# Transformer layer with routed experts: the first expert layer moves from expert order to token order

## The reference

```python
xn = layernorm(x)
# attention, linear, 16 heads of 16
q, k = elu(xn @ Wq + bq) + 1, elu(xn @ Wk + bk) + 1
v = xn @ Wv + bv
kv = einsum('bkhd,bkhm->bhdm', k, v)
att = (einsum('bqhd,bhdm->bqhm', q, kv) / max(sum_k(q . k), 1e-6)) @ Wo + bo
# feed-forward: a shared part for every token ...
swiglu = lambda x: silu(x[..., :512]) * x[..., 512:]
shared = swiglu(xn @ w_in.T) @ w_out.T
# ... and a routed part: one first layer for all experts, two of 8 second layers for each token
h = swiglu(xn @ w1.T)                      # 8192 x 512
w_se = top2(softmax(masked expert logits) * group probability)
routed = sum_e (h * w_se[:, e]) @ w2[e].T  # 8192 x 256
out = x + att + shared + routed
```

## Time and profile before

| | us |
|---|---|
| median of 3 runs | 1070.78 |
| lowest and highest run | 1067.65, 1071.2 |
| the profiled execution, its own time | 1058.75 |
| its span, first to last instruction | 1056.8 |
| stage one ends on PE (last matmul of `y`) | about 609.8 |
| first expert matmul of stage two | 612.65 |

### The profile page before, as it was taken

The page is one execution under the profiler, slowest core; times in us unless marked ns, Lnnn a source line. Parts: engine busy times, 40 slices in busy tenths (PEclk is TensorE's granted clock), DMA queues, the critical chain, the costliest instruction groups (busy, mean ns, idle before and its releaser), DMA issues.

```text
span 1056.8 us, 21589 instructions
## 1 busy us (share of the span) xinstructions
PE 1012.4 (96%) x6662; PEld 910.4 (86%) x6663; DVE 672.9 (64%) x1681; ACT 398.8 (38%) x676; POOL 491.5 (47%) x489
## 2 busy tenths in 40 slices
PE   5999999999999999999999889999999999999996
PEld 5889879888888888898888779999999999999996
DVE  7887797788779778877977634444443444444343
ACT  3454354345445444544444322222222222222221
POOL 5343343534343443334344445555555555555534
PEclk9999999999999999999999899999999999999999
DMA  8012111201211120211111032222222122222321
GB/s 269 24 53 73 52 40 52 72 20 57 68 52 40 52 72 26 64 54 52 40 52 53 12 82 71 64 72 61 69 69 71 63 69 69 63 68 69 65 45 21
DMA packets 55585, 64.55 MB, mean 61 GB/s; under 512 B 18829, under 2 KB 45581, under 8 KB 55568
## 3 DMA queue, kind: packets, MB, share of 16 engines
q1 hardware_dynamic: 42624, 35.86, 11.3%
q0 software_dynamic: 12944, 28.47, 9.9%
HBM read 37.16 MB, written 28.58 MB: 62 GB/s over the span
## 4 chain that ended last, share of the span: by engine, by line
PE 60%; DVE 22%; issue 12%; ACT 3%; DMA 1%; POOL 1%; SPq 0%; DVEq 0%; ACTq 0%; POOLq 0%
PE bank L309 19%; PE bank L310 19%; PE bank L311 18%; DVE xn L715 4%; PE bank L381 3%; DVE stats L701 2%; DVE gated L795 1%; DVE lmax L726 1%; DVE phiq L825 1%; DVE phik L808 1%; PE bank L502 1%; ACT expt L617 1%; ACT expt L619 1%; ACT gated L598 1%; DVE rn L857 1%
## 5 line engine op out<-in xcount | busy, mean ns | idle before, releaser
L598 ACT ACTIVATE gated<-bank 128x512 f32<-128x512 f32 (+1 forms) x140 | 83.0, 593 | 264.2 <-PE bank L311 224.6
L309 PE MATMUL bank<-wexp_hi,h_hi 128*128 x600 | 170.2, 284 | 0.3 <-DVE h_lo L961 0.3
L310 PE MATMUL bank<-wexp_lo,h_hi 128*128 x600 | 168.5, 281 | 0.0
L311 PE MATMUL bank<-wexp_hi,h_lo 128*128 x600 | 168.5, 281 | 0.0
L997 POOL TENSOR_TENSOR h_lo<-gated,h_hi 128x512 fp32r<-128x512 f32 x64 | 83.8, 1309 | 170.5 <-ACT h_hi L602 169.0
L602 ACT CAST h_hi<-gated 128x512 fp32r<-128x512 f32 (+1 forms) x140 | 86.4, 617 | 159.1 <-DVE gated L795 158.4
L795 DVE TENSOR_TENSOR gated<-gated,bank 128x512 f32<-128x512 f32 (+1 forms) x140 | 95.2, 680 | 77.5 <-ACT gated L598 77.5
L971 DVE SCALAR_TENSOR_TENSOR res<-bank,cur,res 128x256 f32<-128x256 f32 x150 | 62.2, 477 | 123.1 <-PE bank L311 120.7
L1058 POOL DMA_INDIRECT out<-res,idx_cur x75 | 74.2, 989 | 102.9 <-DVE res L971 88.9
L309 PE MATMUL bank<-xnT_hi,wexp_hi 128*128 128x512 f32 (+1 forms) x304 | 117.7, 387 | 1.0 <-DVE xnT_lo L952 1.0
L310 PE MATMUL bank<-xnT_lo,wexp_hi 128*128 128x512 f32 (+1 forms) x304 | 117.7, 387 | 0.0
(11 more groups left out here) (171 smaller groups left out, 2506.6 us busy)
## 6 DMA issues: line engine op xcount, KB each, us to landing
xt<-x SPq DMA_DIRECT2D x16, 512.0 KB, 3.6
xn_d<-xn SPq DMA_DIRECT2D x16, 512.0 KB, 2.9
base_d<-res SPq DMA_DIRECT2D x16, 512.0 KB, 4.5
wstage<-w_exp SPq DMA_DIRECT2D x16, 320.0 KB, 4.2
tab_d<-wexp_hi SPq DMA_DIRECT2D x12, 128.0 KB, 5.5
phik<-tab_d SPq DMA_DIRECT2D x76, 2.0 KB
xn<-xn_d,idx_next POOLq DMA_INDIRECT x76, 2.8
res<-base_d,idx_cur POOLq DMA_INDIRECT x76
```

The lines of the kernel that those rows point to most:

```text
L309: e.matmul(to, w_hi, m_hi_, start=first_, stop=False, skip_group_check=free)
L310: e.matmul(to, w_hi, m_lo_, start=False, stop=False, skip_group_check=free)
L311: return e.matmul(to, w_lo, m_hi_, start=False, stop=last_, skip_group_check=free)
L598: act.activation(gated[:, j % 2, 0:cols], bank[gate_bank][:, 0:cols], ACT.Silu).then_inc(sil, 1)
```

## The change

The routed first layer is taken in stage one, in token order, from the transposed tokens that are there already (`routed`, four tiles of 12 matmuls with 512 columns for each sequence). Its gated result (128 x 512 fp32 for a tile) is scattered by POOL to `h_d` in HBM in expert-pair order, with the same positions as the table's rows. The residual + attention + shared part goes straight to the output, in token order. Stage two has only the second layer left: for each tile SP reads the tile's 128 rows of `h_d` in four DMAs, one for each band of 32 partitions, such that a block transpose on DVE (32 x 32 blocks) leaves the whole tile transposed; ACT rounds it, DVE makes the low part, PE takes 24 matmuls of 256 columns, DVE multiplies and adds the two results, and POOL scatters them to the output with an adding DMA. The groups have eight tiles, with one PSUM bank each; there are again 75 tiles. The normaliser of the attention is kept with heads on the partitions (32 rows for each tile), which does away with four transposes, one ACT copy and the shape of the last steps. `xn` shares its memory with `xt`; the residual is loaded a second time into `res`. `table_rows` and the layer norm's statistics come before the third gate on DVE. Tiles' padding rows are zeroed in `h_d` between the stages by 13 DMAs. Cut to its core:

```diff
+    h_d = nc.dram_tensor("h_d", (ROWS, H1), f32, kind="Internal").ap()
...
+        xn = xt
...
+        hs = [phik[:, 0:2, :].rearrange("p t d -> p (t d)"), phik[:, 2:4, :].rearrange("p t d -> p (t d)"),
+              expt[:, 0, :], expt[:, 1, :]]
...
+            def load(b, last):
...
+                    sp.wait_ge(t_done, DC * (b + 1))
+                    sp.dma_start(xt[:, :, :], x_rows(b + 1)).then_inc(x_ld, 16)
...
+                    wait_apart(sp, base_rdy, DC * b)
+                    sp.dma_start(out_rows(b - 1), res[:, :, :]).then_inc(base_st, 16)
+                    wait_apart(sp, base_st, 16 * b)
+                sp.dma_start(res[:, :, :], x_rows(b)).then_inc(r_ld, 16)
+                if first_row(b):
+                    sp.wait_ge(wexp_split, 1)
...
+            def tiles_in(q):
+
+                wait_apart(sp, tab_ld, 16 * TB * q)
+                at = [sp.value_load(info_i[0:1, 2, bass.ds(q * TB + t, 1)], min_val=0, max_val=SENT) for t in range(TB)]
...
+                    sp.dma_start(tab[:, bass.ds(q * TB + t, 1), :].rearrange("p t w -> p (t w)"),
...
+                    wait_apart(sp, tr_done, TB * q + t - 3)
+                    for i in range(4):
+                        sp.dma_start(hb[t][32 * i:32 * i + 32, :].rearrange("p (b f) -> p b f", b=TB),
+                                     h_d[bass.ds(at[t], P), i * P:(i + 1) * P].rearrange("(b p) f -> p b f", b=TB)).then_inc(h_ld[t], 16)
...
+            def routed(t, banks):
+
+                for half in range(2):
+                    for c in range(DC):
+                        mm = mm3(pe, bank[banks[half]][:, :], xnT_hi[:, c, t * P:(t + 1) * P], xnT_lo[:, c, t * P:(t + 1) * P],
+                                 w1_hi[:, c, half * H1:(half + 1) * H1], w1_lo[:, c, half * H1:(half + 1) * H1], c == 0, c == DC - 1)
+                mm.then_inc(rh_done, 1)
...
+
+                hidden(3, (3, 7))
+
+                pe.wait_ge(rsil_rdy, TB * b + 1)
+                pe.wait_ge(rg_rdy, TB * b + 1)
+                routed(1, (0, 1))
+
+                pe.wait_ge(rn_rdy, b + 1)
+                for c in range(DC):
+                    mm = pe.matmul(bank[(6, 2)[c]][:, :], spread[:, c, :], qn_hi[:, 1, :], start=True, stop=True)
+                    mm.then_inc(nb_done, 1)
+
+                pe.wait_ge(sil_rdy, HC * (b + 1))
+                pe.wait_ge(gate_rdy, HC * (b + 1))
...
+                routed(3, (0, 1))
+
+                pe.wait_ge(mlo_rdy, b + 1)
+                pe.wait_ge(qn_rdy, DC * (b + 1))
...
+                    transposes(b + 1)
...
+                tiles = LAST_TILES if last else GT
+                for t in range(tiles):
+                    at = [pe.value_load(info_i[0:1, n, bass.ds(g * GT + t, 1)], min_val=0, max_val=(E - 1) * HC * D)
+                          for n in range(2)]
+                    wait(pe, ysum, GT * g + t - 7)
+                    if first_row(g) and t in (5, 6):
+                        pe.wait_ge(base_rdy, DC * B - 6 + t)
+                    pe.wait_ge(tlo2, GT * g + t + 1)
...
+                        for j in range(HC):
+                            off = at[n] + (W1 + j * D)
...
+                high(b, 2)
+                act.wait_ge(acc_done, b + 1)
+                act.wait_ge(phiq_rdy, DC * (b + 1))
+                routed_silu(b, 0, 0)
+                act.wait_ge(m_done, b + 1)
+                act.copy(m_hi[:, :, :].rearrange("p c n -> p (c n)"), bank[4][:, :]).then_inc(mhi_rdy, 1)
+                silu(b, 3, 3)
+                high(b, 3)
+                routed_silu(b, 1, 0)
...
+                ranks_in(b)
...
+                table_rows(b)
                 if not last:
-                    gate(1, HC * b + 1, 1, sil_rdy, gate_rdy)
...
+                routed_gate(b, 0, 1)
...
+                if not last:
+                    normalise(b + 1)
+                gate(b, 3, 7)
+                if last:
+                    tile_list()
+                routed_gate(b, 1, 1)
...
+                routed_gate(b, 2, 7)
...
+                routed_gate(b, 3, 1)
...
+            def transposed(t, g):
+
+                dve.wait_ge(h_ld[t % TB], 64 * (2 * g + t // TB + 1))
+                wait(dve, tlo2, GT * g + t - 1)
+                dve.transpose(hT[t % 2].rearrange("p j (b k) -> p b j k", b=TB),
+                              hb[t % TB].rearrange("p (b j k) -> p b j k", b=TB, j=HC)).then_inc(tr_done, 1)
+
+            def low(t, g):
+
+                dve.wait_ge(thi2, GT * g + t + 1)
...
+                    wait(dve, out_st[t], 16 * g)
+                    dve.wait_ge(cur_rdy, 2 * g + t // TB + 1)
+                    dve.wait_ge(sw_done, GT * g + t + 1)
+                    add(t, g, 0)
+                    ahead(low, t + 3, g, last)
+                    dve.wait_ge(ystep, GT * g + t + 1)
+                    add(t, g, 1)
+                    ahead(transposed, t + 4, g, last)
...
+                def scatter(d, src, t, done):
+                    pool.indirect_dma_start(d, bass.IndirectOffsetOnAxis(ap=pos_i[:, t:t + 1], axis=0), src, None).then_inc(done, 16)
...
+                low(1, HC * b + 1, hhi_rdy, hlo_rdy)
                 if not last:
                     reciprocal_root(b + 1)
...
+                for t in range(TB):
+                    scatter(tab_d, rows[:, t, :], t, row_st)
                 low(2, HC * b + 2, hhi_rdy, hlo_rdy)
+                wait_apart(pool, rg_rdy, TB * b + 1)
+                scatter(h_d, hs[0], 0, hs_st)
                 low(3, HC * b + 3, hhi_rdy, hlo_rdy)
-                if not last:
-                    table_out()
+                for t in range(1, TB):
+                    wait_apart(pool, rg_rdy, TB * b + t + 1)
+                    scatter(h_d, hs[t], t, hs_st)
...
+            def scatter(g, half, tiles=TB):
+                wait_apart(pool, idxc_rdy, 2 * g + half + 1)
+                for t in range(TB * half, TB * half + tiles):
+                    wait_apart(pool, ysum, GT * g + t + 1)
+                    pool.indirect_dma_start(out, bass.IndirectOffsetOnAxis(ap=idx_cur[:, half, t % TB:t % TB + 1], axis=0), ring[t], None,
+                                            bounds_check=N - 1, oob_is_err=False, compute_op=ALU.add).then_inc(out_st[t], 16)
...
+            def group(g, last):
+                if last:
+                    scatter(g, 0, LAST_TILES)
+                else:
+                    entries(g, 1)
+                    scatter(g, 0)
+                    entries(g + 1, 0)
+                    scatter(g, 1)
```

More of the change, by code:

```diff
@@ new lines, in _ @@
+            rounds(sp, load, B)
+            sp.wait_ge(zero_set, 1)
+            sp.wait_ge(ends_rdy, 1)
+            for n in range(NCLS + 1):
+                if n < NCLS:
+                    g, k = divmod(n, NCLS // 2)
+                    j, i = PAIRS[k]
+                    end = sp.value_load(ends[0:1, 16 * g + 4 * j + i:16 * g + 4 * j + i + 1], min_val=0, max_val=SENT)
+                    tail = bass.ds(end, P)
+                else:
+                    tail = slice(SENT, ROWS)
+                sp.dma_start(h_d[tail, :], zeros).then_inc(zero_st, 16)
@@ L373, in _, with transposes @@
+            tiles_in(0)
+            with sp.Fori(1, NH) as q:
+                tiles_in(q)
         @block.tensor
         def _(pe):
-            def transposes(banks, done, free_sem, free_of, ready, ready_n):
-                pe.wait_ge(ready, ready_n)
+            def transposes(b):
+                pe.wait_ge(xn_rdy, b + 1)
                 for c in range(DC):
-                    wait(pe, free_sem[c], free_of[c])
                     for t in range(TB):
-                        mm = pe.transpose(bank[banks[c]][:, t * P:(t + 1) * P], xn[:, t, c * P:(c + 1) * P], ident)
-                    mm.then_inc(done, 1)
@@ L473, in batch @@
                 mm.then_inc(kvt_done, 1)
[L474 to L487 removed]
+                if first_row(b):
+                    pe.wait_ge(wexp_split, 2)
+                pe.wait_ge(sil_rdy, HC * b + 2)
+                pe.wait_ge(gate_rdy, HC * b + 2)
+                routed(0, (0, 1))
                 if first_row(b):
@@ L778, in table_rows @@
                 wait(dve, row_st, 16 * TB * b)
+                wait(dve, hs_st, 16 * TB * b)
                 dve.wait_ge(rank_rd, b + 1)
@@ L856, in batch @@
[L856 to L868 removed]
+                gate(b, 2, 4)
@@ new lines, in add, with ahead @@
+            def add(t, g, n):
+                wts = cur[:, t // TB, t % TB, :].bitcast(f32)
+                if n == 0:
+                    dve.tensor_scalar(ring[t], bank[t][:, 0:D], wts[:, 1:2], None, ALU.mult).then_inc(ystep, 1)
+                else:
+                    dve.scalar_tensor_tensor(ring[t], bank[t][:, D:2 * D], wts[:, 2:3], ring[t],
+                                             ALU.mult, ALU.add).then_inc(ysum, 1)
+            def ahead(step, t, g, last):
+                if not last or t < LAST_TILES:
+                    if t < GT:
+                        step(t, g)
```

(23 more changed lines are left out.)

517 lines of the change are left out of this document (211 added, 306 removed).

## The result

The changed kernel takes 1088.51 us (median of 4 runs, 1086.56 to 1089.2) against 1069.79 for the kernel before (4 runs, 1067.65 to 1071.2): the ratio is 1.0185, with an interval of 1.0161 to 1.0209. It is slower by 18.7 us. The forecast was 1092 on a basis of 1070.8, slower by 21. The kernel before varies more than the changed one: taken again beside the experiments, its runs lie between 1059.2 and 1074.65 us, with medians of 1059.5 to 1067.9 by group.

The account below looks back on a forecast made before the run. PE's work plus its few waits was taken as the bound. 168 - 4 + 11.5 - 152.3 - 1.7 = +21.5 us gave a span of about 1078, with the 12 us offset 1092; range 1066 to 1115, with rivals 1050 to 1126.

Parts of the forecast that it names:

- the sequencer's 1.5 + 1.9 + 0.36: Stage two, PE's sequencer per tile: register loads 1.5, matmuls 1.9, two waits about 0.3, loop 0.06; 3.8 us.
- SP's queue: Stage two: SP's register loads, waits and DMA issues take 14.7 us for four tiles, 3.7 us for a tile.
- The rule on the sequencer: Stage two: the skill's some 62 ns per matmul, in place of 1.9 us, gives 3.3 us a tile, about 1057 in all.
- rows 4: Profile rows of the kernel before, second layer: register addresses for a tile's eight products cost PE's sequencer 1.9 us.
- Rival A: Stage two: sequencer keeps ahead, PE stays the bound; sequencer and SP at 3.05 us a tile, 1036 us; chance 0.24.
- The point from which it decides: Stage two: under 3.5 us for a tile the change wins.
- the normaliser's matmuls: +0.1: Stage one, PE: matmuls with 128 columns in place of 16, between 0 and +1 us per sequence, taken as +0.1.
- 0.7 for both: Stage one: PE's waits for DVE's third and fourth gates, 0.7 us per sequence together, between 0 and 1.7.
- rival C: Stage one: DVE's chain from second to fourth gate sets the time; at +2 us per sequence 1124 us; chance 0.16.
- Rival B: Stage two: PE's clock falls as it idles a quarter of the time; half the tiles slow, +70, 1162; chance 0.08.
- The transition: Between the stages, last `y` to first expert matmul: 14.4 us in place of 2.9, +11.5.
- The end: From the last matmul's end to the kernel's end: some 6 us with one scatter, 7.7 before with three, -1.7.

Follow-up runs that it names:

- gate_first: Changed kernel with the third gate on DVE moved ahead of the layer norm's statistics, nothing else: 1078.79 us.
- norm_early: Changed kernel with the next sequence's layer norm statistics moved to the head of the sequence, the previous sequence's final adds behind them: 1063.84 us (10 runs).
- before_again: The kernel before, unchanged, profiled a second time: 1067.31 us, span 1065.4.
- dve_order: Changed kernel with DVE's stage-one steps reordered by what PE needs next, and POOL's reciprocal root behind the four table scatters: 1101.56 us.
- pe_keep: Changed kernel with PE's two register values loaded once for eight tiles, the other seven tiles' right experts left out: 1081.1 us.

## Why the prediction was right, and where its steps were off

**The sign and the size.** The chain of reasoning held: +11 for each of 16 sequences is more than stage two gives back, because a tile without the first layer costs 3.7 us and not 2.9. The step that carried it, the sequencer's 1.5 + 1.9 + 0.36, was forecast at 3.80 and measured at 3.71: the loads took 1.5, the matmuls 1.95 and the waits 0.19, so that only the last term was too large. The loop's turn (once for eight tiles) makes one step in eight 4.05, and the others lie between 3.6 and 3.9. SP's queue was forecast at 3.7 and measured at 3.52. The pair of experiments shows that the two queues back each other: had one of them been free, the other would have held the step within 0.2 us of the same place.

**The rule on the sequencer.** The step measured 3.71. By the sum with the rule's figure in place of the row it would have been 3.3 and the forecast 1057. So rows 4, of a queue that ran ahead of the array, were a true price of dispatch. The Trainium skill (TensorE: Matmul & The Clock Gate, section "Wait — 56ns, not 53.3ns?") states some 62 ns for a matmul's dispatch with hardware decode off, a condition that the prediction left out and that no run here shows; with register addresses the rows gave 79 (1.9 us / 24), the changed kernel 81 (1.95 us / 24), and the measured step agrees with the rows.

**Rival A** (3.05 us for a tile) is refuted by the step, and it took two edits at once to reach 2.9. **The point from which it decides** was near: the 18.7 us are 0.25 for each of 75 tiles, so that it lies at 3.71 - 0.25 = 3.46 and not at 3.5.

**Stage one was mis-sized, by two terms of opposite sign.** Forecast +10.5 for a sequence, measured +11.2 (47.52 - 36.36). The step "the normaliser's matmuls: +0.1" failed: from their start to that of the next matmul it is 0.57 us (662.93 to 663.50) for 1.71 (329.05 to 330.76), so -1.1. The matmul behind them, in the kernel before:

```profile
330.76 0.42 PE L472 MATMUL bank<-stay,relut 128*128 128x128 f32 x2
```

And the step "0.7 for both" waits failed: 2.43 was measured, above the bound of 1.7. The second follows from the first and from one more: PE had 3.2 us of cover for the third gate and not 4.3, since the normaliser got shorter, and the gate was ready 5.5 us after the second one and not 4.7, since one step of `table_rows` took 0.86 us beside POOL (L801, at 665.24). The fourth gate, the other half of "0.7 for both", brought no wait over 0.1 us in this sequence. The balance, by the stretches: PE's busy time +9.4 (44.97 for 35.54), forecast at +10.6; its idle time +1.7 (2.55 for 0.82), forecast at -0.1; together 11.2. Three falls of the clock, 1.5 us each, come on top, and a wait of 4.2 us for the router's choice in the first sequence (L476; it is at most 0.28 in the others). So **rival C** was in part the truth, with +1.7 of wait where it had +2; `gate_first` and `norm_early` show that it was the chain, and what it and the falls of the clock behind it cost: 24.7 us.

**Rival B** in part too, and not where it was placed. In the middle of stage two gaps of 0.5 to 1.0 us before each tile left the clock at 1.00 over 230 us. But in stage one the clock fell behind three of the waits of 2.4 us: to 0.74 on the mean of the 6.5 us after 93.53, to 0.50 for some 3 us at 142.71 and again at 477.39, and each time the period was 1.5 us longer, 4 to 5 us together. With waits of 1.4 us at most (`gate_first`) there was no fall. The forecast had a wait of 2.7 us with a fall and of 0.8 without, but took no wait of 2.4 to be there in stage one. A wait of 1.6 us was enough at times: twice in `before_again` (1.56 and 1.57) and three times in `dve_order`, while the first profile of the kernel before has four waits of 1.55 to 1.57 before the transposes and no fall behind them. In stage two the clock fell seven times in `pe_keep`, behind waits of 2.1 to 3.0 us; SP's queue kept its pace of 14.1 us for four tiles, so that the falls cost nothing there. At the start of stage two the clock was 0.64 over 8 us, behind the wait of 12.45, which the forecast left out: the first tile took 5.28 us (799.38 to 804.66) where the next ones took some 2.9. The sequencer, which sets the pace, had a tile in hand: its own step there was 4.27 us and the next five lie between 3.25 and 3.55, so that some 1 us of it may have stayed, by an estimate from these steps.

**The transition**: 12.45 for 14.4. SP's four DMAs for a tile took 1.85 and not 2.3 (0.32 each and some 0.18 between them, where 0.58 was taken for an issue), twice on this path, and they landed some 1.9 us after the last was issued (793.5 to 795.4), where 2.8 was taken from a gather.

**The end**: +2.1 for -1.7. "Some 6 with one" scatter failed: POOL's wait for the last scatter ends 2.8 us after its start, where it was 2.1 in the kernel before, and POOL's DRAIN takes 4.7 for 1.6, which is most of the 3.8 that were missing.

**DVE's transpose**, which no row had shown, took 0.70 us, as taken; with 2.3 us of work for a tile DVE did not set the step of stage two.

**The number.** On the profiled execution the forecast fell short by 9 us (+21.5 for +30.4). That 1092 came within 4 us of 1088.5 is partly luck: the offset of 12 us between the profiled execution and the median, carried over unchanged, was that execution's and not the kernel's (`before_again`: 1067.3, its trace like the median). Without it the forecast would have read 1080 against 1088.5. Against the span of the second profile, 1065.4, the changed kernel's is longer by 21.8, so that how well the sum of +21.5 fits hangs on which execution of the kernel before is taken.

## What to carry to other kernels

When work leaves an engine, ask what its sequencer still has to do for each step: register loads that were hidden under long matmuls become the price of the step once those are gone. Here it was worth 61 us to load four values in one instruction (0.33 us for four, 0.30 for one), without the check of their bounds and with part of SP's loads on another queue. Where an engine's queue is the bound, look for the second queue close behind it before relieving one: here each alone gave 4 to 7 us and both gave 55. And a wait for a gate is a chain's, not a gate's: moving one member forward shifted most of the wait, reordering the chain made it longer, and taking work out to a place with idle time shortened it.

## What was not expected of the hardware

- One register load of four neighbouring values took 0.332 us on PE, of one value 0.301; with the check of its bounds a single one cost the sequencer 0.75.
- A scatter that adds in HBM took POOL 1.54 us to issue against 0.97, and landed in some 4.4 us against 2.5 (medians of the page).
- POOL's DRAIN at the end took 1.625 us in the kernel before (both profiles), 4.678 in every kernel with the adding scatter and 7.501 with the plain one in the same place. Each length is the same to the nanosecond in every profile (nine with the adding scatter, three without), so that it belongs to the program; what sets it stays open.
- A 128 x 128 fp32 step of DVE with operands in SBUF took 2.07 us beside POOL's reciprocal root and low part and 0.35 without them, a factor of 6.
- TensorE's clock fell to its lower level for 3.2 to 3.6 us behind single waits of 1.56 to 1.67 us in five cases, and of 2.4 us in others, but not behind every wait of that length.
- 16 small matmuls with 32-column weights and 128 moving columns took 0.57 us to the next matmul's start; 16 with 128-column weights and 16 moving columns took 1.71.
- In one execution of 3 of one kernel, SP's instructions at the turn of its loop took 0.69 us each and cost 21 us over stage two.
